# Deformable sampling: the row weights made on VectorE instead of ScalarE

## The reference, cut to what matters

```python
sy = off[:, :, :, 0] + kys + hh
sx = off[:, :, :, 1] + kxs + ww
...
val = gather(y0, x0, (1 - dy) * (1 - dx)) + gather(y0, x0 + 1, (1 - dy) * dx) \
    + gather(y0 + 1, x0, dy * (1 - dx)) + gather(y0 + 1, x0 + 1, dy * dx)
patches = val.reshape(Bx, C, KK, Hx, Wx)
out = jnp.einsum('bikhw,oik->bohw', patches, weight.reshape(Cout, Cin, KK))
```

## Time and profile before

| | |
|---|---|
| median of 3 runs | 12056.17 us (12046.54 to 12099.12) |
| profiled execution | 12053.83 us, its span 12051.9 us |
| busy, share of the span | PE 92%, PEld 70%, DVE 81%, ACT 86%, POOL 42% |
| sampling (L884, L831, L836, L1019) | about 630 to 7220 us |

### The profile page before, as it was taken

One profiled execution on the slowest core, in us unless ns is written; L12 is line 12 of the kernel. 1 busy time (PEld: TensorE's weight loads), 2 busy tenths in 40 slices (PEclk: granted clock), 3 DMA queues, 4 the chain that ended last, 5 costly groups with the idle time before them and its releaser, 6 DMA issues. The chain is left out here.

```text
span 12051.9 us, 337397 instructions
## 1 busy us (share of the span) xinstructions
PE 11074.3 (92%) x133078; PEld 8457.9 (70%) x133078; DVE 9815.6 (81%) x14111; ACT 10353.3 (86%) x10426; POOL 5059.6 (42%) x3633
## 2 busy tenths in 40 slices
PE   6689999999999999999999999850899899999999
PEld 4389999999999999999999984420633455555555
DVE  4578888888888888888888886799878788888888
ACT  3299999999999999999999993596778899998998
POOL 0033333333333433343333430133200588888887
PEclk9899999999999999999999995985999899999999
DMA  6488888888888888888888888444544333333332
GB/s 165 129 223 213 214 218 217 218 214 211 215 214 214 217 216 219 218 219 216 215 216 215 219 205 198 136 163 132 171 150 156 116 101 102 108 101 103 101 101 85
DMA packets 818421, 2128.02 MB, mean 177 GB/s; under 512 B 145699, under 2 KB 414369, under 8 KB 674497
## 3 DMA queue, kind: packets, MB, share of 16 engines
q1 hardware_dynamic: 800912, 2072.13, 64.3%
q10 hardware_dynamic: 15120, 30.71, 0.7%
q0 software_dynamic: 832, 3.59, 0.1%
HBM read 1782.85 MB, written 323.30 MB: 175 GB/s over the span
## 5 line engine op out<-in xcount | busy, mean ns | idle before, releaser
L884 PE MATMUL dc_p<-dc_t 96*64 96x90 f32 (+1 forms) x103896 | 4658.9, 247 | 144.9 <-issue 71.7
L884 PEld LDWEIGHTS dc_p<-dc_t 96*64 96x64 f32 x103896 | 4370.8, 136 | 418.1 <-issue 416.4
L955 POOL TENSOR_TENSOR dc_t<-dc_t 128x324 f32<-128x324 f32 (+1 forms) x2885 | 2591.8, 898 | 4028.3 <-DVEq L1043 2738.2
L1019 DVE TENSOR_TENSOR dc_t<-dc_p,dc_t 128x810 f32<-128x810 f32 (+1 forms) x2886 | 3043.5, 1055 | 896.4 <-DVEq L1016 861.1
L831 ACT ACTIVATE dc_t<-dc_t 96x2304 f32<-96x2304 f32 x1447 | 3189.0, 2204 | 105.6 <-ACTq L830 104.5
L836 ACT ACTIVATE dc_t<-dc_t 96x2304 f32<-96x2304 f32 x1446 | 3049.9, 2109 | 0.0
L2545 DVE TENSOR_TENSOR_SCAN ms_t<-ms_t,ms_p 128x512 f32<-128x512 f32 x1728 | 2127.0, 1270 | 283.7 <-PE ms_p L2487 203.7
L2461 POOL TENSOR_TENSOR ms_t<-ms_t 128x1536 f32<-128x1536 f32 x576 | 1987.9, 3456 | 503.3 <-DVE ms_t L2545 499.6
L2497 PE MATMUL ms_p<-ms_t,top_t 128*128 128x512 f32 x3456 | 1774.7, 596 | 0.0
L925 PE MATMUL dc_p<-dc_t 128*128 128x180 f32 (+1 forms) x7488 | 1536.5, 337 | 3.4 <-issue 2.0
L2487 PEld LDWEIGHTS ms_p<-top_t,ms_t 128*128 128x128 f32 x6912 | 850.9, 141 | 966.4 <-issue 693.8
(11 more groups left out here) (258 smaller groups left out, 9527.7 us busy)
## 6 DMA issues: line engine op xcount, KB each, us to landing
dc_t<-sxd SPq DMA_DIRECT2D x1447, 864.0 KB, 6.1
ms_t<-bcd SPq DMA_DIRECT2D x576, 256.0 KB, 3.3
dc_t<-xrT SPq DMA_DIRECT2D x49, 675.0 KB, 9.7
kvd<-wk_t SPq DMA_DIRECT2D x18, 1536.0 KB, 5.1
szd<-mi_t SPq DMA_DIRECT2D x36, 768.0 KB, 4.4
xvd<-mi_t SPq DMA_DIRECT2D x36, 768.0 KB, 4.8
dld<-mi_t SPq DMA_DIRECT2D x36, 768.0 KB, 3.4
ms_t<-dld SPq DMA_DIRECT2D x36, 768.0 KB, 6.8
```

Of the source, the lines that this page charges most:

```text
L884: ins = e.matmul(PT[j % 2][o:o + 64, t // 3, t % 3 * nr * CG:(t % 3 + 1) * nr * CG], HX[:, m // 2 % RP, m % 2, t * 128 + o:t * 128 + o + 6 ...
L955: e.tensor_tensor(ZH[:, n % 4, :, 0:m], z[:, :, 0:m], z[:, :, nr * CG - m:nr * CG], ALU.add)\
L1019: e.tensor_tensor(Zt[:, n % 4, 0:nr * LEN].rearrange("p (b m i) -> p b m i", b=3, i=CG), PT[n % 2][:, :, 0:3 * nr * CG].rearrange("p b (m ...
```

## The change

`row_weights` goes from ACT's program to DVE's. There it is two tensor_scalar instructions for each half: a bitwise or with 0x80000000 on V as uint32, in place, which sets the sign bit and so gives -|V|, and then (x + 1) followed by max with 0, into HY. It stands behind `rows`, at n % 20 = 6, 8, 10 and 12, ahead of `weigh(n + 6)`; for the first tile all four stand ahead of the first `weigh`. The waits go with it: s_hyf, s_rw and s_va2 are taken on DVE now. The rest of ACT's program and the programs of the PE, POOL and SP are the same.

```diff
--- before.py
+++ after.py
@@ -836,38 +836,18 @@
                     e.activation(HX[:, q % RP, :, :], HX[:, q % RP, :, :], ACT.Relu, bias=1.0, scale=-1.0)\
                         .then_inc(s_hx, 2)
 
-                def row_weights(i, step):
-
-                    o = slice(step // 2 * HM * ROWSOF[i % 3], (step // 2 + 1) * HM * ROWSOF[i % 3])
-                    if step % 2 == 0:
-                        e.wait_ge(s_rw, 2).then_inc(s_rw, -2)
-                    if step == 0:
-                        e.wait_ge(s_hyf, 1).then_inc(s_hyf, -1)
-                    if step % 2 == 0:
-                        e.activation(V[:, o], V[:, o], ACT.Abs).then_inc(s_va2, 1)
-                    else:
-                        e.wait_ge(s_va2, 1).then_inc(s_va2, -1)
-                        e.activation(HY[:, i % 2, o], V[:, o], ACT.Relu, bias=1.0, scale=-1.0).then_inc(s_hy, 1)
-
-                for step in range(4):
-                    row_weights(0, step)
                 distance(0)
                 for q in range(AHEAD // 2):
                     distance(q + 1)
                     hats(q)
 
                 def body(b, y2, w):
-                    for n in range(NBB):
-                        i, j = n // NB, n % NB
-                        if n % 2 == 0:
-                            distance((n + AHEAD) // 2 + 1)
-                            hats((n + AHEAD) // 2)
-                        if j in (4, 5, 9, 10):
-                            row_weights((i + 1) % NRB, (4, 5, 9, 10).index(j))
+                    for n in range(0, NBB, 2):
+                        distance((n + AHEAD) // 2 + 1)
+                        hats((n + AHEAD) // 2)
 
                 loops(e, body)
                 e.wait_ge(s_ab, 1).then_inc(s_ab, -1)
-                e.wait_ge(s_hyf, 1).then_inc(s_hyf, -1)
 
             @blk.tensor
             def _(e):
@@ -981,6 +961,20 @@
                                     TAB[:, i % 2, 0:nr].unsqueeze(1).to_broadcast([128, CM // 4, nr]), ALU.add)\
                         .then_inc(s_rw, 1)
 
+                def row_weights(i, step):
+
+                    nr = ROWSOF[i % 3]
+                    o = slice(step // 2 * HM * nr, (step // 2 + 1) * HM * nr)
+                    if step == 0:
+                        e.wait_ge(s_hyf, 1).then_inc(s_hyf, -1)
+                    if step % 2 == 0:
+                        e.wait_ge(s_rw, 2).then_inc(s_rw, -2)
+                        e.tensor_scalar(V[:, o].bitcast(U32), V[:, o].bitcast(U32), 0x80000000, None, ALU.bitwise_or)\
+                            .then_inc(s_va2, 1)
+                    else:
+                        e.wait_ge(s_va2, 1).then_inc(s_va2, -1)
+                        e.tensor_scalar(HY[:, i % 2, o], V[:, o], 1.0, 0.0, ALU.add, ALU.max).then_inc(s_hy, 1)
+
                 def add_up(b, i, conv):
                     e.wait_ge(s_f, 1).then_inc(s_f, -1)
                     total = k.SUM[:, b, conv, :]
@@ -1050,6 +1044,8 @@
                         unload(n)
                         if n % NB in (2, 4, 6, 8):
                             rows((n // NB + 1) % NRB, n % NB // 2 - 1)
+                        if n % NB in (6, 8, 10, 12):
+                            row_weights((n // NB + 1) % NRB, n % NB // 2 - 3)
                         weigh(n + 6)
                         quarter(n + 4)
                         weigh(n + 7)
@@ -1059,6 +1055,8 @@
 
                 for s in range(4):
                     rows(0, s)
+                for step in range(4):
+                    row_weights(0, step)
                 weigh(0)
                 weigh(1)
                 weigh(2)
```

## The result

The changed kernel takes 12135.6 us (median of 15 runs, 12112.7 to 12148.7) beside 12077.0 us of the kernel before (15 runs, 12046.5 to 12099.2): a ratio of 1.0044, 95% interval 1.0035 to 1.0054. By the ratio that is 53 us slower, by the two medians 59, where the forecast had 30 us: the direction is as forecast, but the loss is nearly twice the sum. The profiled execution took 12133.6 us as span, 81.7 more than before's. The sampling stage, from the start of the PE's first sampling to the start of its last transpose (L893, now L873), grew from 6588.2 to 6654.1 us, 65.9 us. The other 16 us lie behind it, in stages that the change doesn't touch, and are differences of one execution.

What follows compares the result with a forecast made beforehand. The PE sets the pace, DVE its only close follower. Five-row tiles lose 20 us with five-row followers, 10 with six-row ones, six-row tiles zero: 30 us on 12053.83, plus 2.3 for the median, 12086 us; range 12045 to 12145.

Steps and rivals of the forecast that it cites:

- own bounds: The forecast case's limits: 12060 us at a price of 0.31 us an operation, and 12115 us.
- rival (b): DVE becomes the bound: each new operation costs 0.88 us (0.80 net), 117 us in all, 12173 us; chance 0.20.
- ACT's work is worth nothing: Sampling stage: removing 171.4 + 171.9 us from ACT costed at zero, since ACT leads the PE by some 8 us.
- The price of the operation: Each of four DVE tensor_scalar a tile, 128x450: taken as 0.48 us, 0.40 net; 0.05 more for 540.
- POOL's turn: At n = 10 and 12 the new DVE operations wait until POOL's addition ends, up to 0.8 us each.
- The ledger: PE loss per five-row tile with five-row follower, n = 6 to 12: 0.23, 0.14, 0.05, 0; 0.42 us, 30 us over all tiles.
- s10: Letter s plus number: start of the PE's sampling of that number in a tile; sampling 10 needs the buffer w8 empties.
- the floor of 0.43: Least time in us from the end of a `weigh` to the PE's sampling that reuses its buffer; spare is time above it.
- rival (a): Nothing shows: the PE's "issue" gaps let DVE catch up; 3 to 5 us lost, 12060 us; chance 0.15.
- (c): ACT was a bound after all, PE idle shrinks: at most 105 us and more, some 11960 us, half 12004; chance 0.07.
- w8: The `weigh` of sampling 8 of a tile on DVE; the late row load lets it start at 2992.64 only.
- A stage longer by more than the PE's waits: Sign that the forecast is wrong: something in the transfers would have moved; no size given.

Runs made afterwards that it cites:

- e3_double: Kernel before with four extra DVE operations of the change's kind and size on scratch memory, ACT still making the weights: 12111.0 us, ratio 1.0040.
- e1_late: Changed kernel with the four row-weight operations on DVE at n = 12, 14, 16 and 18: 12074.9 us, ratio to the kernel before 0.9997.
- e10_second: Changed kernel with the four operations at n = 10, 12, 14 and 16, none at 6 and 8: 12068.4 us, ratio to the kernel before 0.9998.
- e9_first: Changed kernel with the four operations at n = 6, 8, 14 and 16: 12120.9 us, ratio to the kernel before 1.0039.
- e2_tiny: Changed kernel with the four DVE operations cut to 8 elements each, most row weights not computed: 12087.1 us, ratio to the kernel before 1.0012.
- e7_after_early: Changed kernel with SyncE issuing the next tile's row loads at pair 5 of a tile, not its end: 11954.6 us, ratio to the kernel before 0.9894.
- e6_before_early: Kernel before with SyncE issuing the next tile's row loads at pair 5 of a tile, not its end: 11932.8 us, ratio 0.9881.
- e5_rows_act: Kernel before with DVE's rows at n = 4, 6, 12, 14 and ACT's row weights at j = 8, 9, 15, 17: 11931.2 us, ratio 0.9882.
- e4_spread: Changed kernel with rows at n = 4, 6, 12, 14 and row weights at 8, 10, 16, 18: 11918.5 us, ratio to the kernel before 0.9875.
- e8_spread_early: e4_spread with the next tile's row loads issued at pair 5 of a tile: 11925.6 us, ratio to the kernel before 0.9871.

## Why the forecast was right in kind and short in size

**The number.** The forecast was 12086 us, its own bounds 12060 to 12115, its range 12045 to 12145. Measured were 12135.6, inside the range and above the forecast's own bounds. Of the 50 us between, 21 come from the base (12056.2 us was a median of 3 runs, 12077.0 one of 15) and 29 from the loss, 59 by the medians and not 30. The range held because it was kept wide for rival (b), whose mechanism, an operation of 0.88 us in all four places, did not occur. That part of the hit is luck.

**"ACT's work is worth nothing": right.** ACT's idle before L831 rose from 98 to 612 us, and e3_double, which leaves ACT full, loses as much as the change.

**The price of the operation: too high at n = 6 and 8.** I took 0.48 us (0.40 net) between two bounds; it is 0.38 (0.30 net) for 450 elements and 0.43 for 540. The lower bound, 0.31 for 180 elements, lay nearer. The page "VectorE: DVE Perf Modes" of the Trainium skill (its tier table) led to 0.40 as an estimate, and the trace agrees within 0.02 us. Its sum of 15 us, though, would have been further off the whole loss than mine.

**POOL's turn: right in place, larger in size, worth nothing that can be told.** I had up to 0.8 us at n = 10 and 12. Seen were 0.51 and 0.88 in the tile above, 0.82 and 1.19 in six-row tiles, and 0.94 on average for the OR in e1_late. By the Trainium skill, page "SBUF — State Buffer" (section "SBUF: two separate sides"), GpSimd and a DVE instruction in a two-port mode exclude each other; the trace agrees, since the operation at 1798.24 ends 0.25 us after POOL's end at 1798.87. The page's rule speaks of DVE's time, and e10_second shows that this time was spare. One reading was wrong: the L979 at 3040.45 did not find POOL idle. A POOL addition was in progress, and it was this one that took longer, 1.38 us and not 0.76:

```profile
3040.12 1.38 POOL L955 TENSOR_TENSOR dc_t<-dc_t 128x324 f32<-128x324 f32 x1 [0.63 <-POOLq L951]
```

**The ledger: the right operations, about twice too high.** I worked out 0.42 us for a five-row tile with a five-row follower (the first kind), 0.21 for one with a six-row follower (the second), none for six rows (the third). To compare, I split the stage into the run of each sampling (first to last of its 36 records) and the turn between two runs, and took each over the shortest usual length of its place in the tile (the 5% quantile over all kernels). A turn counts as "behind its `weigh`" where the sampling started at most 0.445 us (0.555 for a pair's second) after the end of the `weigh` that freed its buffer. Sums in us, of one profiled execution each ("none": at most one such turn):

| kernel | within runs | turns behind their `weigh` | other turns |
|---|---|---|---|
| before | 128 | 39 | 26 |
| after | 167 | 58 | 35 |
| e3_double | 177 | 48 | 31 |
| e9_first | 171 | 54 | 36 |
| e2_tiny | 146 | 47 | 24 |
| e1_late | 130 | 45 | 31 |
| e10_second | 129 | 44 | 32 |
| e7_after_early | 65 | none | 20 |
| e6_before_early | 53 | none | 19 |
| e5_rows_act | 47 | none | 16 |
| e4_spread | 46 | none | 17 |
| e8_spread_early | 46 | none | 18 |

What the ledger counts belongs in the second column, which grew by 19 us, but about half of that lies ahead of s10, where the change adds nothing and the three kernels named next differ among themselves by as much. Counted at the ledger's places, against the mean of the three kernels with nothing at n = 6 and 8 (before, e1_late, e10_second), the turns ahead of s14, s16 and s18 are longer by 0.07, 0.10 and 0.07 us a tile in the first kind (ledger: 0.23, 0.14 and 0.05), by 0.07 together in the second (0.21), and not in the third. That makes 15 us where the ledger had 30. A reason is the tile that I read: it is later than most. In the kernel before the median over the 48 tiles of its kind, from the end of the `weigh` to s14 and s16, is 0.85 and 1.50 us, so over the floor of 0.43 the spare is usually 0.42 and 1.07 us and not 0.17 and 0.43; about a quarter of the tiles are as tight as mine. That the loss hangs on n = 6 and 8, as the ledger had it, is shown by e9_first and e10_second.

**What was left out: delay within the runs.** The stage grew by 66 us, and 39 of them are in the first column. This is the step that the forecast had wrong: it let the PE lose time only where a sampling waits for its buffer, took the "issue" gaps inside a run of sampling matmuls as fixed, and in rival (a) even as relief for DVE. They are not fixed. The gaps of over 0.3 us alone rose from 89 to 115 us. The first column is 167 to 177 us in the three kernels with full operations at n = 6 and 8 and late row loads, and at before's 128 in e1_late and e10_second. By the same comparison the runs of s18 and s19 are longer by 0.31 and 0.13 us in the first kind and those of s16 and s17 by 0.20 and 0.13 in the second, behind the very stretch that the ledger is about. So this delay is in part a product of what DVE does at n = 6 and 8. That is shown.

How it comes about is not. The gaps have a mark in the records of packets. Of those over 0.3 us from 650 to 7050 us, 84 of 86 before and 90 of 91 after ended 1.2 to 1.7 us after the end of a transfer of the queue that brings instructions, where a moment taken at random does so in 7% of cases:

```profile
q8 instruction: 1080, 17.69, 0.7%
```

(packets, MB: 16 KB each, as many in the kernel after, whose page this line is from). These transfers were not slower than the others (median 1.10 and 1.09 us against 1.18); they came later after the one before (8.8 and 9.3 us against 7.2 and 7.4 of all). The PE's gap at 1795.38 and that of before at 3013.53 split a sampling in mid-run, where the code has no wait. A reading that fits: a PE whose queue has been held up by semaphores asks for its next instructions too late. No run isolates it, and it has to explain e7_after_early too, where the first column is 12 us above e6_before_early's although no sampling but one starts so close behind its `weigh` in either. So this stays open.

**The rivals.** (a), nothing shows, falls with the interval of 1.0035 to 1.0054. (b) had DVE at 0.88 us four times and 117 us; in the kernel after such prices were seen at n = 10 and 12 (medians of 0.5 to 1.2 us) and at n = 6 and 8 in a few cases only, and at 10 and 12 they cost nothing that can be told. (c) fell with e3_double. The largest effect was in none: DVE's wait at `rows`, which I had named as what makes w8 late and yet never priced, starts the lateness that all of it rests on. Without it the stage is 123 to 130 us shorter (6465.6 and 6458.2 against 6588.2), although the PE had waited visibly for only 34 us behind its semaphore. By the table 75 to 82 us of that are within the runs, 39 in the turns behind their `weigh`, the rest in the other turns.

**The marks.** DVE was 281 us busier over the whole execution (290 forecast). ACT was 264 us less busy and not 343: its records overlap by about 0.1 us, and busy time counts a moment once. The PE's wait behind L859 rose to 45 us (60 forecast), with idle before s16 but only 0.05 us before s14. "A stage longer by more than the PE's waits" was named as the sign that something else had moved, and it came (66 us against 35), though the transfers' amount did not change; whether the moment of the instruction transfers is cause or company is the open question above.

## What to carry to other kernels

Before work is added to an engine that follows the pace setter closely, find the wait that starts its lateness: issuing a load earlier, or moving its consumers later, was worth 1.2% here, and the added work cost 0.44%. The same operations cost nothing that can be told six samplings further on in the tile, though the OR took 0.94 us there and not 0.53; the place counts, not the busy time. And one tile's timeline is one sample: its spare of 0.17 us stood beside a median of 0.42. Idle time that a profile calls "issue" is not a constant of the kernel: it moved from 70 us to 92 and to 22 with the lateness of another engine.

## What the runs showed of the chip that I had not expected

A bitwise_or on 128x450 words took 378 ns and the addition with a maximum 377 (the shortest of each), as fast as each other; 90 more elements cost 0.05 us. POOL's turn adds the same to a short operation as to a long one: at n = 12 of a five-row tile with a five-row follower the addition took 0.88 us in the kernel after and 0.66 in e2_tiny, cut to 8 elements, where they take 0.38 and 0.16 alone (medians). So L978 of e2_tiny, on 8 elements, took 643 ns on average over 286.
